# Softmax denominators transposed, inverted once per query and head, and spread again by two products with the identity

## What is computed

```python
q = split_heads(query @ Wq.T + bq)
k = split_heads(key @ Wk.T + bk)
v = split_heads(value @ Wv.T + bv)
scores = jnp.einsum('bhqd,bhkd->bhqk', q, k) / np.sqrt(HEAD_DIM)
weights = jax.nn.softmax(scores, axis=-1)
out = jnp.einsum('bhqk,bhkd->bhqd', weights, v)
out = out.transpose(0, 2, 1, 3).reshape(b, -1, D_MODEL)
return out @ Wo.T + bo
...
x = x + jnp.tanh(g_xattn[0]) * _L0_xattn_ref(_layernorm(x, axis=-1), ctx_1024, ctx_1024, ...)
x = x + jnp.tanh(g_ffn[0]) * _L0_ffn_ref(_layernorm(x, axis=-1), ...)
```

## Time and profile before

| what | value |
|---|---|
| three runs, us | 1031.39, 1027.44, 1034.13 |
| median, us | 1031.39 |
| profiled execution, us | 1031.14 |
| its span, us | 1029.3 |
| granted TensorE clock, mean | 0.968 |
| PE / PEld / DVE / ACT / POOL busy | 88% / 64% / 71% / 57% / 51% |

### The profile page before, as it was taken

One profiled execution on the slowest core, in us unless ns is written; L12 is line 12 of the kernel. 1 busy time (PEld: TensorE's weight loads), 2 busy tenths in 40 slices (PEclk: granted clock), 3 DMA queues, 4 the chain that ended last, 5 costly groups with the idle time before them and its releaser, 6 DMA issues.

```text
span 1029.3 us, 32569 instructions
## 1 busy us (share of the span) xinstructions
PE 903.9 (88%) x13088; PEld 654.4 (64%) x13088; DVE 729.9 (71%) x1575; ACT 588.3 (57%) x1076; POOL 520.7 (51%) x666
## 2 busy tenths in 40 slices
PE   3887789898999898999999999999999999999974
PEld 1354467676777667677666776676666666666653
DVE  5676666877858778686876867777787878787722
ACT  1165446565575755657556575666657575756550
POOL 5544435643535455354654557666666575762202
PEclk9998889999999999999999999999999999999985
DMA  5334451222212222221655757577666666666200
GB/s 139 91 89 136 133 148 40 79 69 81 74 52 69 73 76 78 71 66 56 141 114 106 133 103 160 125 154 140 138 152 129 145 133 140 133 122 110 42 1 19
DMA packets 100290, 104.47 MB, mean 101 GB/s; under 512 B 28250, under 2 KB 93100, under 8 KB 100140
## 3 DMA queue, kind: packets, MB, share of 16 engines
q1 hardware_dynamic: 98722, 102.07, 42.6%
q10 hardware_dynamic: 1418, 0.32, 0.2%
HBM read 35.89 MB, written 0.46 MB: 35 GB/s over the span
## 4 chain that ended last, share of the span: by engine, by line
PE 57%; DVE 24%; ACT 9%; issue 7%; DMA 1%; POOL 0%; SPq 0%; ACTq 0%; POOLq 0%; DVEq 0%
DVE mx L1034 13%; PE pO L1162 13%; PE pMX L1183 10%; PE pST L1141 9%; PE pKV L1228 6%; PE pKV L1219 6%; PE pFH L1350 5%; PE pFY L1282 3%; ACT P L757 2%; DVE rden L976 2%; ACT HR L809 2%; ACT L757 2%; DVE HR L932 2%; PE pFY L1286 1%; DVE ysc L1005 1%
## 5 line engine op out<-in xcount | busy, mean ns | idle before, releaser
L1034 DVE TENSOR_REDUCE mx<-pMX 112x1 f32<-112x500 f32 x768 | 487.1, 668 | 134.1 <-PE pMX L1183 131.2
L757 ACT ACTIVATE P<-pST 125x448 f32<-125x448 f32 x768 | 389.5, 542 | 291.1 <-PE pST L1141 286.1
L1183 PE MATMUL pMX<-kop,qmax 48*112 48x500 f16 (+1 forms) x768 | 285.1, 410 | 48.3 <-DVE mx L1034 38.3
L1141 PE MATMUL pST<-qexp,kop 50*128 50x112 f16 (+2 forms) x3072 | 267.7, 216 | 21.4 <-issue 11.7
L1141 PEld LDWEIGHTS pST<-qexp,kop 50*128 50x128 f16 (+2 forms) x3072 | 184.5, 101 | 87.5 <-issue 33.2
L1162 PE MATMUL pO<-P,V 125*17 125x112 f32 x6144 | 188.8, 264 | 0.0
L1183 PEld LDWEIGHTS pMX<-kop,qmax 48*112 48x112 f16 (+1 forms) x768 | 97.7, 130 | 123.1 <-DVE mx L1034 60.2
L614 POOL CAST khi<-kfull 128x500 f16<-128x500 f32 x96 | 57.9, 603 | 206.4 <-ACT kfull L773 204.9
L1162 PEld LDWEIGHTS pO<-P,V 125*17 125x17 f32 x6144 | 138.8, 98 | 34.2 <-issue 18.7
L616 POOL TENSOR_TENSOR klo<-kfull,khi 128x500 f16<-128x500 f32 x96 | 109.0, 1135 | 7.8
L705 POOL TENSOR_TENSOR Clo<-C,Chi 128x500 f16<-128x500 f32 x93 | 105.9, 1139 | 7.5
(11 more groups left out here) (147 smaller groups left out, 1110.2 us busy)
## 6 DMA issues: line engine op xcount, KB each, us to landing
C<-in_ctxT SPq DMA_DIRECT2D x31, 750.0 KB, 5.5
kop<-maskop SPq DMA_DIRECT2D x48, 437.5 KB
kop<-khi SPq DMA_DIRECT2D x192, 62.5 KB
kop<-khi SPq DMA_DIRECT2D x96, 125.0 KB
kop<-klo SPq DMA_DIRECT2D x96, 62.5 KB
kop<-klo SPq DMA_DIRECT2D x48, 125.0 KB
maskin<-in_mask SPq DMA_DIRECT2D x8, 656.2 KB, 6.0
qexp<-qmax SPq DMA_DIRECT2D x16, 182.0 KB
```

Of the source, the lines that this page charges most:

```text
L757: nc.scalar.activation(P[0:KP, slot, h * 4 * T:(h + 1) * 4 * T], pST[0:KP, h, 0:4 * T], ACT.Exp, scale=EXP_SCALE).then_inc(exp_done, 1)
L1034: nc.vector.tensor_reduce(mx[:, s % 2, c, p:p + 1], pMX[0:T, m % 2, 0:CW], AX.X, ALU.max).then_inc(max_done, 1)
L1141: mm = nc.tensor.matmul(pST[0:keys.stop - keys.start, h, i * T:(i + 1) * T], kop[rows, b, slot, keys], qexp[rows, b, slot, :, :].rearrange ...
L1183: nc.tensor.matmul(pMX[0:T, m % 2, 0:CW], qmax[rows, b, slot, :, :].rearrange("r j q -> r (j q)"), kop[rows, b, slot, c * CW:(c + 1) * CW] ...
```

## The change

The use "sum" becomes two products with OM as the weights and four columns of ones (`sel` is 128x4 now): they give the denominators with queries on partitions, 112x8. DVE takes the reciprocal of these 112x8 values. POOL copies them into `rows`, each value 32 times along a row (112 x 2 x 128). A new use "share" of pFY at the end of slot 6, in every step that has a "sum", multiplies `rows` by the identity, two products, which turns them back to 128x224 in PSUM. In slot 7 DVE multiplies OM by them straight from PSUM into ON. POOL's multiplication and addition are gone. The value bias is multiplied by the output weights once, in step 2 slot 8, and added to `tbo`. "y" no longer waits for POOL; it waits for DVE's multiplication through the bank.

```diff
 def fy_uses(s):
     uses = []
+    if s == 2:
+        uses.append((8, "bias", LAYERS))
...
     if is_batch(s - 2):
-        uses.append((5, "sum", 1))
+        uses += [(5, "sum", 1), (6, "share", 1)]
...
-        sel = sb("sel", [128, 128])
+        sel = sb("sel", [128, 4])
...
-        bvm = sb("bvm", [128, LAYERS, 2, 2, S])
+        bvm = sb("bvm", [128, LAYERS, 2, T])
...
-        rden = sb("rden", [128, 2 * T])
+        rden = sb("rden", [T, PAIRS])
+        rows = sb("rows", [T, 2, 128])
...
                 if is_batch(s - 2):
-                    l = layer_of(s - 2)
                     pool.wait_ge(fy_free, upto(fy_uses, s, "sum", True))
                     apart(pool)
-                    if s >= 4:
-                        pool.wait_ge(fy_ready, upto(fy_uses, s - 2 + (s + 1) % 2, "y"))
+                    if s >= 3:
+                        pool.wait_ge(fy_ready, upto(fy_uses, s - 1, "share"))
                         apart(pool)
-                    link(nc.gpsimd.tensor_tensor(OM[:, s % 2, :], OM[:, s % 2, :], rden[:, :], ALU.mult))
-                    nc.gpsimd.tensor_tensor(ON[:, :, :, s % 2, :].rearrange("p r j q -> p (r j) q"),
-                                            OM[:, s % 2, :].rearrange("p (n q) -> p n q", q=S),
-                                            bvm[:, l, :, :, :].rearrange("p r j q -> p (r j) q"),
-                                            ALU.add).then_inc(on_done, 1)
+                    nc.gpsimd.tensor_copy(rows[:, :, :].rearrange("t r (g i) -> t (r g) i", g=4),
+                                          rden[:, :].unsqueeze(2).broadcast_to([T, PAIRS, 32])).then_inc(rows_done, 1)
...
+                for l in range(LAYERS):
+                    for r in range(2):
+                        nc.vector.tensor_scalar(bvm[:, l, r, :], ones[:, 0:T], bvE[:, l, r:r + 1], None, ALU.mult
+                                                ).then_inc(init_l, 1)
...
-                        nc.vector.reciprocal(rden[:, :], pFY[:, 0:2 * T]).then_inc(fy_free, 1)
+                            dve.wait_ge(rows_done, st.at(lambda s: s - 2))
+                        nc.vector.reciprocal(rden[:, :], pFY[0:T, 0:PAIRS]).then_inc(fy_free, 1)
+                    elif use == "share":
+                        if s >= 4:
+                            dve.wait_ge(fy_ready, upto(fy_uses, s - 2 + (s + 1) % 2, "y"))
+                        nc.vector.tensor_tensor(ON[:, :, :, s % 2, :].rearrange("p r j q -> p (r j) q"),
+                                                OM[:, s % 2, :].rearrange("p (n q) -> p n q", q=S),
+                                                pFY[:, 0:2 * T].rearrange("p (n q) -> p n q", q=S),
+                                                ALU.mult).then_inc(fy_free, 1)
+                    elif use == "bias":
+                        for l in range(LAYERS):
+                            nc.vector.scalar_tensor_tensor(out=tbo[:, l, :], in0=pFY[0:T, l * D:(l + 1) * D],
+                                                           scalar=gains[0:T, l:l + 1], in1=tbo[:, l, :],
+                                                           op0=ALU.mult, op1=ALU.add).then_inc(fy_free, 1)
...
-                        mm = nc.tensor.matmul(pFY[:, 0:2 * T], sel[:, :], OM[:, s % 2, :], start=True, stop=True)
+                        for r in range(2):
+                            mm = nc.tensor.matmul(pFY[0:T, 4 * r:4 * (r + 1)], OM[:, s % 2, r * T:(r + 1) * T], sel[:, :],
+                                                  start=True, stop=True)
+                    elif use == "share":
+                        pe.wait_ge(rows_done, st.at(lambda s: s - 1))
+                        for r in range(2):
+                            mm = nc.tensor.matmul(pFY[:, r * T:(r + 1) * T], rows[:, r, :], ident[0:T, 0:T],
+                                                  start=True, stop=True)
+                    elif use == "bias":
+                        pe.wait_ge(init_l, 13)
+                        for l in range(LAYERS):
+                            for r in range(2):
+                                mm = nc.tensor.matmul(pFY[0:T, l * D:(l + 1) * D], bvm[:, l, r, :], woE[:, l, r, :],
+                                                      start=(r == 0), stop=(r == 1))
                     elif use == "y":
-                        pe.wait_ge(on_done, st.at(lambda s: s - 1))
```

More of the change, by code:

```diff
@@ L216, in pool_links @@
         n += 3
-    if is_batch(s - 2):
-        n += 1
     if has_a(s):
@@ L406, in build @@
         statf_done, xnf_done = sem("statf_done"), sem("xnf_done")
-        on_done = sem("on_done")
+        rows_done = sem("rows_done")
         logit_done, gexp_done, gate_done = sem("logit_done"), sem("gexp_done"), sem("gate_done")
@@ L596, in _ @@
                                         base=0, pattern=[[-1, 128]], channel_multiplier=1).then_inc(init_p, 1)
[L597 to L600, removed]
+            nc.gpsimd.affine_select(out=sel[:, :], in_=sel[:, :], compare_op=ALU.not_equal, fill=1.0, base=-PR,
+                                    pattern=[[-32, 4]], channel_multiplier=1).then_inc(init_p, 1)
             def links_before(s):
@@ L891, in late_constants @@
                 dve.wait_ge(init_a, 1)
+                for l in range(LAYERS):
+                    for r in range(2):
+                        nc.vector.tensor_scalar(bvm[:, l, r, :], ones[:, 0:T], bvE[:, l, r:r + 1], None, ALU.mult
+                                                ).then_inc(init_l, 1)
                 for j in range(2):
-                    for l in range(LAYERS):
-                        for r in range(2):
-                            nc.vector.tensor_scalar(bvm[:, l, r, j, :], ones[:, 0:S], rowmask[:, j:j + 1],
-                                                    bvE[:, l, r:r + 1], ALU.mult, ALU.mult).then_inc(init_l, 1)
                     nc.vector.tensor_scalar(headmask[:, :, j, :], ones[:, :].rearrange("p (r q) -> p r q", r=2),
@@ L901, in late_constants @@
                                             ALU.mult).then_inc(init_l, 1)
-                dve.wait_ge(init_l, 17)
+                dve.wait_ge(init_l, 13)
             def links_before(s):
@@ L974, in from_fy @@
                         if s > 2:
-                            dve.wait_ge(on_done, st.at(lambda s: s - 2))
-                        nc.vector.reciprocal(rden[:, :], pFY[:, 0:2 * T]).then_inc(fy_free, 1)
+                            dve.wait_ge(rows_done, st.at(lambda s: s - 2))
[12 more added lines that the diff above has]
+                                                           op0=ALU.mult, op1=ALU.add).then_inc(fy_free, 1)
                     elif use == "y":
@@ L1058, in step @@
                         if s >= 4:
-                            dve.wait_ge(on_done, st.at(lambda s: s - 3))
+                            dve.wait_ge(fy_free, upto(fy_uses, s - 2, "share", True))
                         nc.vector.tensor_tensor(OM[:, s % 2, :], pO[:, 0:2 * T],
@@ L1191, in step @@
                 if s == 3:
-                    pe.wait_ge(init_l, 17)
+                    pe.wait_ge(init_l, 13)
                     pe.wait_ge(f_in, 16 * 5)
```

## The result

The changed kernel takes 1043.09 us (median of four runs, 1040.13 to 1046.0) against 1031.47 for the kernel before (four runs, 1027.44 to 1034.13): ratio 1.0099, with a 95% interval of 1.0065 to 1.0134. The forecast was 1040.0, its range 1025 to 1047. The profiled execution took 1046.0 us, span 1044.2, so 14.9 us more than the span before.

A forecast was written before the change was run, and what follows sets the result against it. TensorE (PE), 88% busy and 57% of the chain, was taken as the bound, with DVE's relief mostly absorbed. The step terms, value bias and last step came to +8.85 us on about 1031 us: 1040.0 us, range 1025 to 1047.

The forecast's parts named there:

- Odd steps, +0.485 each: Odd steps 3 to 29, 14 of them: share costs PE 0.485 us each, DVE's gain and the sum's are lost; +6.8 us.
- w1a: Four f32 products on PE, eight passes in 0.97 us, used to price the two products of share at 0.485 us.
- Sum: The denominators' products on PE: two at the router product's 0.17 us make 0.34 against 0.45 today, 0.11 us saved.
- Even steps of layer 0, -0.15 each: Even steps 4 to 14, six: PE's 0.43 us wait is spent on share, the later copy comes earlier; -0.9 us.
- Even steps of layer 1, +0.265 each: Even steps 20 to 30, six: share's 0.485 us less the 0.22 us stall after the reciprocal; +1.6 us.
- the old stall: PE's wait after the reciprocal in layer 1's even steps, 0.22 us, expected to be won back.
- the POOL part: Per step, two POOL operations of 0.67 us go out and a copy of 0.31 us (bound 0.61) comes in, hidden.
- Steps 16 and 18, +0.375 each: Two even steps with w1a and without a stall: share's 0.485 us less the sum's 0.11; +0.75 us.
- Copy, reciprocal, multiplication: Prices per step: POOL's copy 0.31 us (bound 610 ns), DVE's reciprocal 203 ns, DVE's multiplication from PSUM 378 ns.
- Value bias and the start: Value bias once in step 2: eight f32 passes 0.97 us, 0.76 saved on DVE; between -0.8 and +1.0, taken +0.5 us.
- Steps 31, 32 and 33: Steps 31 and 32 pay 0.375 us each; step 33's way from reciprocal to y shortens from 3.37 to 2.45, -1.0 with the sum.
- The forecast's mechanism: Share costs PE its full price in odd steps; in even steps PE's waits of 0.43 and 0.22 us behind the reciprocal offset it.

The follow-up runs named there:

- e1: The changed kernel with the two products of share made as transposes, one f32 pass each instead of two; 1036.29 us, ratio 1.0021 to the kernel before.
- e2: The changed kernel with the two products of share issued twice, same result; 1056.64 us (one run).
- e5: The kernel before with only the reciprocal cut from 128x224 to 112x8, most of the division left out; 1031.47 us, ratio 0.9985.
- e4: The kernel before with only the value bias moved to step 2, so POOL has one operation less per step; 1034.02 us, ratio 1.0003.
- e7: The changed kernel with POOL starting a step's last context split only after DVE has written cc; 1042.3 us, ratio 1.0102 to the kernel before.
- e9: The kernel before with POOL starting a step's last context split only after DVE has written cc; 1030.14 us, ratio 0.9972.
- e0: The changed kernel run once more without edits, for a second profile (also e0_after_again); 1046.83 us (one run).
- e3: The changed kernel with share cut to one tiny 16-bit product, all waits kept and the division left out; 1039.25 us, ratio 1.0058 to the kernel before.
- e8: e1 with POOL starting a step's last context split only after DVE has written cc; 1031.39 us, ratio 0.9987 to the kernel before.

## Why the prediction was right, and where it was not

- *Odd steps, +0.485 each.* Right: 0.43 us from the share to the query product, 0.45 in the step, and e1 and e2 scale it with the records. w1a was a fair price, 0.04 too high (0.24 is its price for a product; a record is 0.12, and the prediction's sentence mixes the two). DVE's gain is lost there, as said: e5's odd steps do not move, and DVE idles ahead of ON and qhi.
- *Sum.* 0.11 saved was taken from the router product; 282.16 - 281.77 = 0.39 against 0.45, so 0.06. In odd steps it is lost, as said.
- *Even steps of layer 0, -0.15 each.* Right, -0.11, and by the mechanism named: the wait behind the reciprocal (-0.42 by e5) pays for most of the share.
- *Even steps of layer 1, +0.265 each.* The steps 20 to 28 grew by 0.51, so this term was mis-sized by about half, and in these five steps the mechanism was another: e4 and e5 grow by as much with no share at all. The share less the old stall, +0.24, shows only where the lock does not reach: in e7 against e9 and in step 30. The failed step is the POOL part: it weighed what goes out and what comes in only for whether the share must wait, and not what POOL's being 0.7 us earlier collides with. It is 5 x 0.245 = 1.2 us in all, and no more because cc meets the cast in the odd steps as before.
- *Steps 16 and 18, +0.375 each.* +0.86 and +0.39: the second right, the first not; e7 and e0 have it too (+0.85). The timeline of PE in step 16 shows where it arises, before:

```profile
530.24 0.38 PE L1183 MATMUL pMX<-kop,qmax 104*112 104x500 f16 x1
530.55 0.38 PE L1141 MATMUL pST<-qexp,kop 50*128 50x112 f16 x8
530.86 0.42 PE L1183 MATMUL pMX<-kop,qmax 104*112 104x500 f16 x1
```

and after:

```profile
536.74 0.38 PE L1190 MATMUL pMX<-kop,qmax 104*112 104x500 f16 x1
537.05 0.37 PE L1148 MATMUL pST<-qexp,kop 50*128 50x112 f16 x4
537.35 0.70 PE L1254 MATMUL pFY<-ident,rows 112*128 112x112 f32 x4
537.98 0.37 PE L1148 MATMUL pST<-qexp,kop 50*128 50x112 f16 x4
538.27 0.42 PE L1190 MATMUL pMX<-kop,qmax 104*112 104x500 f16 x1
```

  The share parts two groups of four score products that had run as one group of eight; from maximum to maximum it is 1.53 us instead of 0.62. The price taken from w1a holds no such parting. That it is the parting that costs the rest was not tested.
- *Copy, reciprocal, multiplication.* 399, 194 and 389 ns against 310 (bound 610), 203 and 378. The copy is hidden, the wait for it 1.1 us in the whole run.
- *Value bias and the start.* No price can be given, nor one for steps 2 and 3. The first OM comes at 87.1 us before and 90.0 after; it is at 86.7 to 90.2 in the other traces, and the half clock falls differently there in each. e4 with the moved bias is at 1.0003 of before, with 2.5 us of the lock in it.
- *Steps 31, 32 and 33*, predicted together +0.375, +0.375 and -1.0: -0.64, +0.37, and -0.42 in what follows the last OM. The first and the last repeat in e0 and e7; step 32 depends on the clock. Step 31 went the other way than forecast: DVE's relief alone wins 0.74 there (e5), a gain that the term put at nothing. In step 33 the way from the reciprocal to the y product went from 3.37 to 2.66 us, forecast 2.45, as the share took 1.18 and not 1.01; the new sum ran at half clock there and the old one at full clock, 0.24 longer.

The forecast's mechanism, PE pays where it has no gap and not where DVE made one, stood up in the odd steps and in layer 0's even ones. Added up over steps 5 to 31 (13, 22 and 28, which held half clock, by e0's lengths) and what follows the last OM, the change is +8.2 us, where the forecast's terms for the same stretch give +7.3. That this is so near is in part luck: the lock's 1.2 and step 16's 0.5 stand against step 31's -1.0. The rest of the 11.6 lies in the start, in step 32 and in stretches of half clock, which differ from one execution to the next, and is not attributed. The profiled execution's 1046.0 holds 3.5 us more in steps 13, 22 and 28, by their difference to the steps beside them.

Not settled: the cause in step 16, and what step 3 and the start would be at the same clock. Nor was a share tried that costs PE no product at all.

## What to carry to other kernels

Read the gain of a lighter engine from the waits that end on it, not from its busy time: 37.5 us less on DVE were worth at most 0.42 us in the steady even steps of one layer and nothing in the steady odd ones, while 0.10 to 0.11 us per record on PE came through in full in the odd steps of layer 0. Work that is moved to an engine without gaps costs its full price, so ask for its fewest passes (transposes halve the share). When an off-path engine gets faster, look what its next operations now run beside: POOL early by 0.7 us cost 0.5 us in each of five steps, because a small DVE operation then ran to the end of a longer POOL operation.

## What the runs showed of the hardware

**A DVE operation blocked by POOL.** cc, a DVE operation of 112x8 elements, takes 0.17 us alone and 0.26 to 1.10 us beside POOL, from one trace to the other. Wherever the POOL operation beside it had more than 0.1 us left, cc ended 0.02 to 0.03 us behind it. It looks like a slow operation in the groups (290 ns mean) and shows no wait.

**The clock near the end.** DVE and POOL run out of work in step 32, and there the granted clock falls to 0.5 (1.2 of 2.4 GHz); in the windows ahead of the fall PE was busy 13.10 and 11.64 of 15 us. Windows of the changed kernel's first profile (us, busy of PE, PEld, DVE, ACT, POOL, then the granted clock):

```profile
985.00:1000.00 15.00, 13.10 (x274) 9.84 (x276) 5.75 (x24) 10.50 (x23) 0.40 (x1) 1.00 0.01 2
1000.00:1015.00 15.00, 12.37 (x184) 9.17 (x176) 1.38 (x2) 8.58 (x15) 0.00 (x0) 0.77 0.01 2
```

and of e0_after_again, the same kernel:

```profile
985.00:1000.00 15.00, 11.64 (x250) 8.66 (x246) 3.63 (x19) 11.52 (x22) 0.40 (x1) 1.00 0.01 2
1000.00:1016.00 16.00, 14.85 (x156) 10.88 (x156) 1.55 (x3) 6.49 (x13) 0.00 (x0) 0.54 0.00 1
```

In the first the clock comes back within step 32, in the second it stays low: 22.84 and 25.79 us for that step. Over the twelve profiles step 32 takes 21.5 to 22.8 us in six and 25.8 to 26.5 in the other six (e0, e3, e4, e7, e8 and e9). What decides it was not found. Some 3 to 4 us hang on it, so a median of a few runs is blunter here than the step lengths.

**Half clock in the middle.** In ten of the twelve profiles the clock also falls one to three times in steps 4 to 31: in step 4 in six of them, else mostly at other places each time. The changed kernel, with a window ahead of and behind the stretch (columns as above):

```profile
430.00:438.00 8.00, 6.59 (x94) 4.80 (x92) 5.01 (x11) 4.34 (x8) 3.01 (x4) 1.00 0.47 149
438.80:442.40 3.60, 3.60 (x41) 2.64 (x41) 0.80 (x2) 1.30 (x3) 0.33 (x1) 0.53 0.20 68
442.40:450.00 7.60, 7.01 (x114) 5.41 (x117) 6.68 (x17) 4.16 (x9) 4.13 (x7) 1.00 0.12 31
```

PE was busy 6.59 of the 8 us ahead of it. In steps 13, 22 and 28 here and step 9 in e0 such a stretch makes the step 1.0 to 1.6 us longer. What starts it was not found.
